# Spreading a decoder's steps over batches and reordering the first loads in a float32 attention + quantised-layer kernel

## What is computed

```
x = x + attention(layernorm(x), ctx, mask, wq, wk, wv, wo)    # softmax(rope(q) rope(k)^T / sqrt(128) + mask) v, then wo
x = x + layer(layernorm(x))                                   # out = x_norm @ W4^T + bias
# W4[o, i] = lut4[o, code], where bit p of code is a bit of qweight[p, o, i // 32]
```

## Time and profile before

| | us |
|---|---|
| median of 3 runs | 2468.26 |
| lowest, highest | 2468.23, 2469.3 |
| the profiled execution | 2468.72 |
| its span (first to last instruction) | 2466.9 |

### The profile page before, as it was taken

How to read it: one execution, slowest core, us unless ns; L and a number is a source line. 1 busy time by engine, 2 the same in 40 slices (tenths; PEclk the granted TensorE clock), 3 DMA queues, 4 the chain that set the end, 5 groups by cost and what they waited for, 6 DMA issues and landing times.

```text
span 2466.9 us, 36225 instructions
## 1 busy us (share of the span) xinstructions
PE 2451.5 (99%) x13158; PEld 2118.3 (86%) x13158; DVE 1505.7 (61%) x3582; ACT 1141.8 (46%) x2499; POOL 454.9 (18%) x682
## 2 busy tenths in 40 slices
PE   8999999999999999999999999999999999999999
PEld 7998999988888888888888888888888888888887
DVE  7787777555556565565565655555565655565554
ACT  5555545454545454555554444444444444443110
POOL 1000001222222222222222222222222222222211
PEclk9999999999999999999999999999999999999999
DMA  6466568222222222222245412212121111214211
GB/s 245 160 203 198 177 218 273 80 72 87 64 86 69 78 78 77 86 69 78 69 149 189 145 60 61 73 64 67 54 73 60 61 61 61 73 56 157 91 69 52
DMA packets 178464, 255.39 MB, mean 104 GB/s; under 512 B 15600, under 2 KB 114160, under 8 KB 178288
## 3 DMA queue, kind: packets, MB, share of 16 engines
q1 hardware_dynamic: 178288, 253.08, 31.3%
HBM read 181.73 MB, written 71.30 MB: 103 GB/s over the span
## 4 chain that ended last, share of the span: by engine, by line
PE 96%; DVE 2%; ACT 1%; DMA 1%; issue 0%; POOL 0%; SPq 0%; ACTq 0%; DVEq 0%
PE bank L744 28%; PE bank L821 28%; PE bank L760 7%; PE bank L866 7%; PE bank L793 7%; PE bank L683 6%; PE bank L706 6%; PE bank L781 5%; PE bank L655 1%; PE bank L644 0%; DMA residual<-in_ctx 0%; PE bank L771 0%; PE bank L664 0%; DVE residual L1428 0%; DVE acts_split L1343 0%
## 5 line engine op out<-in xcount | busy, mean ns | idle before, releaser
L744 PE MATMUL bank<-acts_split,weights_split 128*128 128x512 f32 (+1 forms) x3360 | 769.9, 379 | 0.0
L821 PE MATMUL bank<-weights_split,small_split 128*128 128x512 f32 x3072 | 741.3, 390 | 2.3 <-DVE small_split L1652 2.2
L821 PEld LDWEIGHTS bank<-weights_split,small_split 128*128 128x128 f32 x3072 | 573.8, 188 | 121.0 <-DVE small_split L1652 2.6
L744 PEld LDWEIGHTS bank<-acts_split,weights_split 128*128 128x128 f32 x3360 | 576.8, 189 | 97.6
L1775 POOL TENSOR_SCALAR probs<-probs,row_numbers 128x256 f32<-128x256 f32 x512 | 241.3, 484 | 1331.6 <-DVE row_numbers L1642 1331.6
L1631 DVE CUSTOM_DVE_ANT_0 probs<-bank,mask_tile 128x256 f32<-128x256 f32 x512 | 197.2, 422 | 255.8 <-PE bank L760 243.3
L1148 ACT ACTIVATE probs<-probs,row_numbers 128x256 f32<-128x256 f32 x512 | 256.6, 502 | 50.6 <-DVE row_numbers L1637 46.6
L1164 ACT ACTIVATE small_split<-bank 128x512 fp32r<-128x512 f32 x127 | 75.9, 597 | 404.2 <-PE bank L793 404.2
L1768 POOL TENSOR_TENSOR rope_x<-rope_x,sin_t 128x512 f32<-128x512 f32 (+1 forms) x140 | 168.1, 1201 | 486.5 <-ACT rope_x L1131 485.8
L1603 DVE SCALAR_TENSOR_TENSOR rope_a<-bank,cos_t 128x512 f32<-128x512 f32 (+1 forms) x140 | 90.4, 646 | 272.2 <-ACT rope_x L1131 272.2
L760 PEld LDWEIGHTS bank<-small_split 128*128 128x128 f32 x1536 | 217.7, 190 | 20.5 <-issue 0.5
(11 more groups left out here) (114 smaller groups left out, 2373.9 us busy)
## 6 DMA issues: line engine op xcount, KB each, us to landing
raw<-in_L_xattn_wq SPq DMA_DIRECT2D x61, 512.0 KB, 4.4
raw<-in_L_xattn_wo SPq DMA_DIRECT2D x60, 512.0 KB, 3.5
k_scratch<-small_split SPq DMA_DIRECT2D x64, 256.0 KB, 2.3
v_scratch<-small_split SPq DMA_DIRECT2D x32, 512.0 KB, 2.9
x_scratch<-raw SPq DMA_DIRECT2D x64, 256.0 KB, 2.8
acts_split<-x_scratch SPq DMA_DIRECT2D x32, 512.0 KB, 6.3
mask_tile<-in_mask_BxSxS_ff SPq DMA_DIRECT2D x64, 256.0 KB, 3.5
small_split<-k_scratch SPq DMA_DIRECT2D x64, 256.0 KB, 2.6
```

Of the source, the lines that this page charges most:

```text
L744: last = pe.matmul(query_bank(j)[:, 0:wide], wq_s[:, h, c, a, :], xT[:, c, m, b * S:b * S + wide], start=c == 0 and i == 0, stop=c == C - ...
L821: last = pe.matmul(out_ps[part][:, :], o_s[:, a, u % 2 * S + t * P:u % 2 * S + (t + 1) * P], wo_s[:, h, m, n * BANK:(n + 1) * BANK], start ...
```

## The change

It does four things.

1. First loads: the context of batch 0 comes in two DMAs of 512 KB and the first key weights in one, in the order context half 0, keys, context half 1. The rope tables are issued after weight piece 2 instead of piece 1. ACT and DVE split two quarters of the context before the keys. PE turns the identity 24 times (`WARM`) right after the identity is there, into a bank that nothing reads.
2. In batch 0 one weight piece per key group is split (pieces 3 to 10), and five after the loop, with V0's low half ahead of the last.
3. The decoder's operations are laid out by tables: `CARRY[b][g]` is what batch `b` does in group `g` for the tile before, `OWN[b][g]` what it does for its own tile. Batch 1 takes over six operations (11 to 16), batch 6 one. `TURN_AT` goes from 3, 1, 1, 1, 1, 1 to 6, 5, 5, 4, 3, 2 for batches 1 to 6, and the second half goes from two groups later to the groups 7, 7, 7, 7, 6, 5 (`SECOND_AT`). With `TURN_AT` move the PE's turning, `full_bit0` (one group earlier) and D0's split and store. SP's loads of the table (`LUT_AT`) and of the next context (`CTX_AT`) get groups of their own.
4. Near the end of stage B `row_factor` moves one unit later and `row_write` two.

The diff, cut to its core:

```diff
-    FIRST_PIECES = (range(3, 4), range(4, 5), range(5, 7), range(7, 8), range(8, 10), range(10, 11), range(11, 13),
-                    range(13, 14))
+    WARM = 24
+    FIRST_PIECES = tuple(range(3 + g, 4 + g) for g in range(HKV))
+    CARRY = {1: ((11,), (12, 13), (14,), (15,), (16,)), 2: ((12, 13), (14,), (15,), (16,)),
+             3: ((13,), (14,), (15,), (16,)), 4: ((14,), (15,), (16,)), 5: ((15,), (16,)), 6: ((16,),)}
+    OWN = {1: {5: (0,), 6: (1,), 7: (2,)},
+           2: {4: (0,), 5: (1,), 6: (2,), 7: (3,)},
+           3: {4: (0,), 5: (1,), 6: (2, 3), 7: (4,)},
+           4: {3: (0,), 4: (1,), 5: (2, 3), 6: (4,), 7: (5,)},
+           5: {2: (0,), 3: (1,), 4: (2,), 5: (3,), 6: (4,), 7: (5, 6)},
+           6: {1: (0,), 2: (1,), 3: (2,), 4: (3,), 5: (4,), 6: (5, 6), 7: (7,)}}
+    V_OPS = 9
+    LUT_AT = {1: 2, 2: 1, 3: 1, 4: 0, 5: 0, 6: 0}
+    CTX_AT = {1: (2, 4), 2: (4, 6), 3: (4, 6), 4: (5, 6), 5: (4, 5), 6: (4, 6)}
-    TURN_AT = [None, 3] + [1] * (NB - 3)
+    TURN_AT = [None, 6, 5, 5, 4, 3, 2]
+    SECOND_AT = [None, 7, 7, 7, 7, 6, 5]
...
-            first_context(0, first_ctx_in[0])
-            first_keys(0, first_wk_in)
-            first_context(1, ctx_in[0])
-            first_keys(1, a_raw_in[0])
-            first_context(2, first_ctx_in[1])
-            first_context(3, ctx_in[1])
+            load_context(0, 0)
+            load_split(0)
+            load_context(0, 1)
...
-                        if g == TURN_AT[b] + 2:
+                        if g == SECOND_AT[b]:
                             store_weights(b - 1, D1)
-                        if g in (4, 6):
+                        if g == LUT_AT[b]:
+                            sp.wait_ge(dq_step, (b - 1) * DQ_STEPS + LEAF7)
+                            sp.dma_start(lut_t, lut_v[b]).then_inc(lut_in, 16)
+                        if g in CTX_AT[b]:
...
             pe.wait_ge(ident_ok, 1)
+            for _ in range(WARM):
+                pe.transpose(x_ps[1][:, 0:P], ident[:, :], ident[:, :])
...
-            first_context_high(0, first_ctx_in[0])
-            first_keys_high(0, first_wk_in).then_inc(first_hi, 1)
-            first_context_high(1, ctx_in[0])
-            first_keys_high(1, a_raw_in[0]).then_inc(w_hi, 1)
-            first_context_high(2, first_ctx_in[1])
-            first_context_high(3, ctx_in[1])
+            context_high(16, 0)
+            context_high(16, 1)
+            first_keys_high(0).then_inc(first_hi, 1)
+            first_keys_high(1).then_inc(w_hi, 1)
+            context_high(16, 2)
+            context_high(16, 3)
...
-                    if not last and g == TURN_AT[b] + 2:
+                    if not last and g == SECOND_AT[b]:
                         weights_high(b - 1, D1)
...
-                    if before is not None and g == 0:
-                        pick(2, B, C_, steps=before)
-                    elif before is not None and g == 1:
-                        pick(3, A, B, last=True, steps=before)
-                    at = g - TURN_AT[b] + 1
...
+                    for op in CARRY[b][g] if g < len(CARRY[b]) else ():
+                        decode(b - 1, op)
+                    for op in OWN[b].get(g, ()):
+                        decode(b, op)
...
+                op = max(op for ops in OWN[b].values() for op in ops) + 1
+                for k in range(op, op + 4):
+                    decode(b, k)
                 values_low(V0)
...
-                if u == NU - 6:
+                if u == NU - 5:
                     row_factor(0)
                     row_factor(1)
+                if u == NU - 4:
                     row_write(0)
```

More of the change, by code:

```diff
@@ L1389, in weights_low @@
                 staged_low(staged_count(tile, i), staging(tile, i)[0], w4_ps[i - D0])
-            def batch(b, first=False, last=False, before=None):
-                steps = Steps(dve, dq_step, b * DQ_STEPS)
-                A, B, C_, D_ = range(4)
[L1395 to L1433, removed]
@@ new lines, in _, with spread_bits @@
+            decoding = [Steps(dve, dq_step, tile * DQ_STEPS) for tile in range(NB)]
+            def spread_bits(tile):
+                dve.wait_ge(planes_in, 16 * (tile + 1))
+                if tile:
+                    dve.wait_ge(w4_ready, tile)
+                for s in range(8):
+                    done = dve.tensor_scalar(mask_words[:, s * P:(s + 1) * P], planes, s, 0x01010101,
+                                             ALU.logical_shift_right, ALU.bitwise_and)
+                decoding[tile].mark(done)
@@ L1435, in values_low, with batch @@
+            def batch(b, first=False, last=False):
                 def values_low(i):
@@ L1440, in batch @@
                     weights_low(b - 1, D1)
[L1441 to L1446, removed]
+                    for op in range(6):
+                        decode(b, op)
                     values_low(V0)
-                    leaf(3, D_)
-                    pick(1, C_, D_)
+                    decode(b, 6)
+                    decode(b, 7)
                     values_low(V1)
@@ L1471, in batch @@
                     if last:
[L1472 to L1486, removed]
-                        else:
-                            pick(2, B, C_)
+                        decode(b, 8 + g)
                         continue
@@ L1556, in batch @@
                     values_low(V3)
-                    assert steps.n == DQ_STEPS
+                    assert decoding[b].n == DQ_STEPS
                     return
-                if before is not None:
-                    leaf(3, D_)
-                    pick(1, C_, D_)
-                pick(2, A, C_)
-                leaf(4, B)
-                leaf(5, D_)
-                if before is None:
-                    pick(1, B, D_)
+                op = max(op for ops in OWN[b].values() for op in ops) + 1
+                for k in range(op, op + 4):
+                    decode(b, k)
                 values_low(V0)
-                if before is not None:
-                    pick(1, B, D_)
                 if b in K_ROW:
                     x_low(K_ROW[b], 0, x_ps[0])
-                leaf(6, C_)
-                steps.wait(but=1)
-                leaf(7, D_)
-                pick(1, C_, D_)
+                for k in range(op + 4, op + 7):
+                    decode(b, k)
                 values_low(V1)
@@ L1578, in batch @@
                     x_low(K_ROW[b], 1, x_ps[1])
-                pick(2, B, C_)
-                pick(3, A, B, last=True)
+                for k in range(op + 7, op + V_OPS):
+                    decode(b, k)
                 if b in V_ROW:
@@ L1588, in batch @@
                 values_low(V3)
-                assert steps.n == DQ_STEPS
-            before = batch(0, first=True)
-            batch(1, before=before)
-            for b in range(2, NB - 1):
+            batch(0, first=True)
+            for b in range(1, NB - 1):
                 batch(b)
```

145 lines of the change are left out of this document (84 added, 61 removed).

## The result

The changed kernel takes 2472.59 us (median; 2470.28 to 2473.93), the one before beside it 2468.24: ratio 1.0017, 95% interval 1.0010 to 1.0024. It is 4.3 us slower, 0.17%; the forecast was 2467.7, with a range up to 2471.0. So this trace explains only a part, and the rest is read from others.

A forecast was written before the change was run, and what follows sets the result against it. PE was taken as the bound, busy 2451.5 of 2466.9 us. Start -2.8, end of B -2.0, batch 2 -0.5, batch 1 +2.6, batches 3 to 5 +2.2 sum to -0.5: 2467.7 us, range 2462.3 to 2471.

The forecast's parts named there:

- the sum: Whole kernel: all gains and losses together give -0.5 us against the earlier profiled execution, 2467.7 on the median's scale.
- The staging buffer: Batch 1: stores of both weight halves through the values' buffer make V0 late; PE waits 2.6 us (2.0 to 3.6).
- Batches 4 to 6 have room: Values of batches 4 to 6: the staging chain of stores costs PE no wait there.
- The start: Batch 0: larger loads and an early clock rise begin key group 1 at 12.3; net 2.8 us gained (1.0 to 4.5).
- The key loops: Key loops: batch 2 gains 0.5 us from a vanished wait; row stores and picks in batches 3 to 5 lose 2.2.
- End of stage B: Near the end of stage B: moved row work removes PE's 1.91 us wait; gain 2.0 us (1.6 to 2.1).
- E + 6.5: Batch 1: landing time of D0's store, counted from E, the end of PE's group 7; landing takes 3.6 us.
- E + 9.5: Batch 1: time of D1's store, counted from the end of PE's group 7; landed at E + 13.1.
- (a): Rival: staging and row waits don't bite, as stores land sooner or steps have slack; -5.3 us, 2463.0; chance 0.25.
- (b): Rival: DVE becomes the bound of the key loops in some ten carried groups; +6, 2473.7; chance 0.07.
- (c): Rival: load rate stays at 258 GB/s and transposes don't raise the clock; start gains about 0.8, 2469.7; chance 0.18.

The follow-up runs named there:

- apart: The changed kernel with a second staging buffer for the second half of the turned weights alone: 2464.27 us, -4.4 against the kernel before.
- again: The changed kernel run and traced once more, nothing altered: 2472.30 us, +4.1 against the kernel before.
- end: The kernel before with only the row work at the end of stage B moved later: 2466.26 us, -2.0 against before.
- decode: The changed kernel with its first loads, transposes and split order and the end of stage B put back as before: 2478.82 us, +10.6 against before.
- endfill: The kernel before with 15 identity transposes in the 1.9 us idle time at the end of stage B: 2467.85 us, -0.8 against before.
- start: The kernel before with only the new first loads, the 24 transposes and the order of the first splits: 2467.95 us, -0.3 against before.
- best: The kernel before with the new start and the new end of stage B, decoding as before: 2464.72 us, -3.2 against before.
- look2: The changed kernel traced again, nothing altered, to explain the gap between profile and median: 2473.19 us.
- look4: The changed kernel, nothing altered, the last of three more traces on the gap between profile and median: 2473.01 us.

## Why the prediction was wrong

By the trace the change costs 1.6 us where the sum said -0.5; by the medians 4.3. Three steps failed. The staging buffer was priced at 2.6 us, in batch 1 alone: "Batches 4 to 6 have room" was wrong, and what a late V0 delays had no term. From the keys of batch 1 to the values of batch 7 the changed kernel's trace takes 326.0 us and that of `apart` 319.0, so the waits that a second buffer takes away cost 7.0. The start was taken at 2.8 us, from a late execution, and is worth less on the median. And the clock behind a wait had no term. The key loops, forecast at +1.7, cost nothing (-0.5), which hides a part of it in the sum.

- **Start, forecast -2.8.** In the trace -2.64 at the keys of batch 1, with group 1 at 11.46 (12.3 taken, 11.1 to 13.5 as bounds; 11.46 to 12.69 in the five traces) and V0's wait for piece 10 at 1.29 (1.0). From 2 to 6 us the loads moved 342 GB/s (326 in `again`), and under the 256 KB loads 258 to 279 (before, `end`, `decode`): between the two rates of the earlier trace rows, so larger loads brought a part of the difference. The step that failed is the comparison: I took the earlier trace rows for the kernel's start, and it was one execution with a late rise of the clock. That -2.64 came so near is luck: the keys of batch 1 begin 1.3 to 1.4 us earlier in `end` and `endfill` than in the trace of before, and 0.4 to 0.9 later in the other four traces of the changed kernel than in this one. By the medians the start gives 0.3 (`start`) to 1.2 (`best` less `end`).
- **End of stage B, forecast -2.0.** Right: -2.04 in the trace, -2.0 in `end`. What I didn't have is that the idle time there also brings the clock down in two executions of three.
- **Batch 1, forecast +2.6.** Mechanism and place right, and each step within 0.2 us up to D1's store: with group 7 left at 79.37, D0 landed at 86.08 (E + 6.5 is 85.87) and D1 was issued at 88.93 (E + 9.5 is 88.87). The term mis-sized is the landing: 4.20 us for 3.6, so V0's low half came 0.7 later, and PE waited 3.26 us for 2.6, inside the bounds given. The third group comes 3.4 later than before, counted from the first.
- **Batches 4 to 6 "have room": wrong.** In batch 4 D1 was stored at 233.92 and landed in 4.90:

```profile
233.92 4.90 DMA w_scratch<-small_split
...
240.27 11.18 PE L691 MATMUL bank<-acts_split,small_split 128*128 128x512 f32 x48 [0.89 <-DVE small_split L1388]
```

I chained D0 and D1 for batches 1 to 3 and didn't for 4, where D1 also comes at group 7. +1.05.
- **What a late V0 delays, left out.** Behind ACT's wait stand the row's copies, its store and the next context's splits. Batch 3's keys began 0.95 us later by this alone, batches 2 and 5 by 0.4 and 0.7. I had named what is queued behind that wait only as far as `rope_high(7)` and V0. The chain in batch 2, from the row's store to the context's split (L914) and the keys of batch 3:

```profile
143.75 3.54 DMA x_scratch<-raw
...
153.00 0.62 ACT small_split L914
...
154.48 0.59 PE bank L714 x3
```

- **Key loops.** Batch 1 -0.37 (no term), batch 2 -0.60 (-0.5 forecast), batch 3 +0.53 (+0.5), batch 4 +0.27 (+0.8), batch 5 -0.31 (+0.9). The places were right:

```profile
169.54 3.14 PE L714 MATMUL bank<-small_split,weights_split 128*128 128x256 f32 x24 [0.43 <-DVE probs L1244]
...
217.86 1.09 PE L672 MATMUL bank<-ident,residual 128*128 128x128 f32 x8 [0.25 <-DVE residual L1428]
...
271.54 6.02 PE L714 MATMUL bank<-small_split,weights_split 128*128 128x256 f32 x48 [0.56 <-DVE rope_a L1244]
```

In batches 4 and 5 PE came later itself, by the delays above, and the same DVE work had more time; that this is why they cost less is argued, not tested.
- **The clock behind a wait: no term at all.** I priced waits at their length. The one in batch 1 brings the clock down in most executions, 1.2 to 1.3 us on top in `look2` to `look4`. With the late landings and later starts it makes the 2.3 us between profile and median.
- **Rivals.** (a), that the waits don't bite, fell. (b), DVE as the bound, fell: with DVE's work as it is `apart` is 4.4 us faster than before. (c) was half right: the start is worth less than it looks, but by the comparison and not by the rate.

## What to carry to other kernels

When work is moved later, follow the buffer that it shares, not only the engines: each store through it costs its landing, here mostly 3.5 to 5 us, and whoever comes next on the buffer waits for all before it. Here a second buffer at the right step gave 8.5 us, and the one other order that was tried 4.2. Price a wait of TensorE above its length, and before a term is taken from one trace of the kernel before, ask whether its start is typical.

## What the runs showed of the hardware

- Idle time of 1.9 us, after more than 2 ms of dense matmuls, was followed by 3.4 us at the lower clock in about two of three executions; in five of the seven traces with a gap of 3.2 to 3.5 us it fell for 3.4 to 6.8 us, from 1.1 us before the gap's end to 0.6 after it. The Trainium skill, page "TensorE: Matmul & The Clock Gate", section "HAM oscillation — how this bites in real kernels", describes such falls behind waits for a DMA; the traces agree, and show them for shorter waits than its rule warns of.
- Turning an identity in such a gap held the clock up (a mean of 1.0 in 41 of the 43 executions of the four filled runs).
- Without transposes at the start the clock rose at 9.8 to 16.8 us in the traces, with them at 4.5 to 7.9.
- A 512 KB store of a staged half took 3.5 to 4.9 us to land in one trace of the changed kernel (60 to 345 us, median 3.8) and up to 5.9 in another, the same instruction in the same kernel. The Trainium skill, page "DMA: Bandwidth & Descriptors", section "Latency and other measured facts", gives the access to HBM under high load as 2 us; with 512 KB at 410 GB/s that is an estimate of 3.3 us, below the landings of the halves shown above (3.56 to 4.90).
